# Down products h_hi·[w_hi | w_lo] 512 columns wide, their right half gated by ScalarE and added by GpSimd; another order at the projections' end

## Chip, cores, metric

One core of a Trainium2 chip runs the kernel. The metric is the device time of one execution in microseconds (us), the lower the better. The five engines are called TensorE (PE), VectorE (DVE), ScalarE (ACT), GpSimd (POOL) and SyncE (SP, which only issues transfers here).

## What is computed

One decoder layer on a float32 input x of 16 x 128 x 256 (16 batches, 128 positions, 256 features), with three blocks, each followed by a residual sum and a layer norm:

```python
x = layernorm(x + attention(x))        # q, k, alpha: 512 wide; v: 256 wide; a scan over the 128 positions
x = layernorm(x + experts(x, ctx, itok))
x = layernorm(x + ffn(x))              # 256 -> 1024 (two, silu gate) -> 1024 -> 1024 -> 256

def experts(x, weights, ensembles, proj_in, proj_out):   # E = 8 experts, hidden 512
    h = relu(einsum('edi,bsi->bsed', proj_in, x))
    o = einsum('eid,bsed->bsei', proj_out, h)
    gate = einsum('bks,bkse->bse', weights, one_hot(ensembles, E))
    return einsum('bsei,bse->bsi', o, gate)
```

All 8 experts are computed for every token, and each output row is multiplied by its gate.

## The kernel before

**Split products.** TensorE multiplies in the format fp32r. To keep float32 accuracy, each operand is stored as a high part (the value rounded to fp32r) and a low part (the rest), and each product is three matmuls: hi·hi, lo·hi and hi·lo, summed in one PSUM bank. `three()` lists them and `product()` issues them. High parts come from ScalarE (a copy that rounds), low parts from GpSimd or VectorE (a subtraction).

**Every engine's order is written out by hand.** Each engine has one in-order program, and they meet only at counting semaphores (`wait_ge`, `then_inc`). An instruction that waits holds everything behind it on its engine. Tokens are handled as t = 0..15 (a batch of 128 rows each), in groups g of J = 4.

**Projections (11 to 90 us).** For each token TensorE computes alpha, q and k (18 matmuls of 512 columns), in banks 0 to 2 or 3 to 5 by the token's parity; `values(g)` computes v for a whole group, after token 1 in group 0 and after the first token of the others, and needs the low parts of all four tokens of its group. The high and low parts of x for token t + 4 are made in turn t: `high_half` on ScalarE and `low_half` on GpSimd stood behind the other work of the turn. VectorE adds the bias (L1000), sums softplus (`a_sum`) and q·k (`b_sum`); ScalarE does abs, exp, ln and copies q and k out of PSUM; GpSimd multiplies q·k (L490).

**Tables (90 to 112 us).** The sums of a and b are transposed by TensorE, a chain of short VectorE operations makes one coefficient for each row (`c_tok`), rows are added and normed (`residual`, `norm_means`), while TensorE does the output products of attention. Behind them TensorE issues IDLE = 36 products of a unit matrix that nobody reads (L810), and then transposes the normed rows of group 0 (`turned(0)`, L816, L817).

**Experts (114 to 481 us).** 32 units, each one expert for one group of 4 tokens. `up` makes one of 4 chunks (128 hidden features x 512 tokens) of a unit's hidden layer: 6 matmuls of 512 columns (L741), in bank 0 or 1. ScalarE's `relu` writes the high part hx_hi (L647), VectorE's `low` the low part hx_lo (L1123). `down` makes the 128 x 256 output of one token: for each of the 4 chunks hi·hi, hi·lo, lo·hi of 256 columns (L845), in bank 2 or 3 by parity. VectorE's `gated` multiplies it by the gate and adds it to the token's row in x_tok (L1130). TensorE alternates: up of the next unit's chunk c, down of this unit's token c. Before `up` of chunk c TensorE waits for `low` of chunk c - 2; before `down` of token j for `gated` of token j - 2.

The first 8 units go group by group through experts 0 and 1 (`step`, two units per step, to 217 us). Meanwhile VectorE sums, norms and splits the later groups (`rows_added`, `norm_apply`, `halves_x`) and makes gates (L968). The other 24 go by pairs of experts (`pair`, 8 units each). There VectorE also takes in a piece of the next block's weights in the first two turns of a unit (`take_piece`: L1174 copy, L1176 compare) and makes one gate per turn (not in the last pair). Twice a pair ScalarE rounds the weights of the coming expert (`expert_high`, after units 1 and 5), and GpSimd subtracts them into wx_lo in four pieces (`expert_low`, L507). GpSimd had nothing else to do here except a root (`root`, L510) per group.

**Feed forward (481 to 806 us)**, in 4 groups, then the last norm and the output.

## Time and profile before

| | |
|---|---|
| median of 3 runs | 816.55 us (815.99 to 817.0) |
| the profiled execution | 814.71 us |
| its span, first to last instruction | 812.8 us |
| TensorE busy | 790.0 us (97%) |
| VectorE, ScalarE, GpSimd busy | 457.9, 306.5, 102.6 us |
| mean granted TensorE clock | 0.998 |

A matmul's record is longer than the time it takes of the engine, as matmuls overlap; what one costs is the distance between the starts of two in a row. The busy time of an engine counts overlapped time once.

### The profile page before, as it was taken

The page shows a single profiled execution, that of the slowest core. Times are in us where ns is not written, and L with a number is a line of the kernel's source. Part 1 is how long each engine was busy: PE and PEld are TensorE (multiplying, and loading weights), DVE is VectorE, ACT ScalarE, POOL GpSimd, SP SyncE. Part 2 cuts the span into 40 slices and gives each one's busy share as a digit, 9 for nine tenths or more (in the row PEclk, how much of TensorE's full clock was granted, in tenths as well). Part 3 has the DMA queues.
Part 4 walks back from the last instruction along what each step waited for, and adds up shares of the span by engine and source line. Part 5 has one row for each costly group of instructions (what it writes and reads, how often), then busy time and mean ns, then how long its engine had stood idle before and what let it go on. Part 6 is the DMA issues. An engine that isn't in the chain of part 4 may idle for free.

```text
span 812.8 us, 12974 instructions
## 1 busy us (share of the span) xinstructions
PE 790.0 (97%) x4414; PEld 689.5 (85%) x4414; DVE 457.9 (56%) x1122; ACT 306.5 (38%) x551; POOL 102.6 (13%) x102
## 2 busy tenths in 40 slices
PE   5999899999999999999999999999999999999996
PEld 4877789999999998999999988888888888888885
DVE  3677858886576676767666554324532453245214
ACT  6677632222232322323232235432643264326331
POOL 3676230001120100202020000000000000000000
PEclk9999999999999999999999999999999999999999
DMA  8500000000412122121311000000000000000000
GB/s 328 203 2 0 1 1 2 2 1 27 130 36 95 53 78 73 44 91 52 104 45 46 15 7 0 1 1 7 19 0 0 6 19 0 0 6 21 0 1 29
DMA packets 15587, 31.46 MB, mean 39 GB/s; under 512 B 1584, under 2 KB 6064, under 8 KB 15280
## 3 DMA queue, kind: packets, MB, share of 16 engines
q1 hardware_dynamic: 15536, 30.82, 11.7%
q8 instruction: 27, 0.44, 0.2%
q14 instruction: 24, 0.20, 0.1%
HBM read 28.72 MB, written 2.10 MB: 38 GB/s over the span
## 4 chain that ended last, share of the span: by engine, by line
PE 93%; DVE 3%; issue 2%; DMA 1%; ACT 1%; SPq 0%; POOL 0%; DVEq 0%; POOLq 0%
PE bank L741 37%; PE bank L921 29%; PE bank L845 22%; PE bank L936 3%; PE bank L810 1%; DMA wp_lo_f<-in_wproj 1%; DVE hx_lo L1123 0%; PE bank L864 0%; PE bank L865 0%; PE bank L817 0%; DVE xT_lo L1118 0%; PE bank L816 0%; DVE xf_lo L1192 0%; DVE sp L975 0%; DVE b_tok L983 0%
## 5 line engine op out<-in xcount | busy, mean ns | idle before, releaser
L647 ACT ACTIVATE hx_hi<-bank 128x512 fp32r<-128x512 f32 x128 | 76.7, 599 | 262.9 <-PE bank L741 262.8
L845 PE MATMUL bank<-wx_hi,hx_lo 128*128 128x256 f32 x512 | 144.9, 283 | 0.0
L845 PE MATMUL bank<-wx_lo_r,hx_hi 128*128 128x256 f32 x512 | 144.8, 283 | 0.0
L845 PE MATMUL bank<-wx_hi,hx_hi 128*128 128x256 f32 x512 | 144.3, 282 | 0.0
L1123 DVE SCALAR_TENSOR_TENSOR hx_lo<-bank,hx_hi 128x512 fp32r<-128x512 f32 x128 | 88.3, 690 | 86.5 <-ACT hx_hi L647 86.1
L741 PE MATMUL bank<-xT_hi,wx_hi 128*128 128x512 f32 x256 | 101.7, 397 | 2.2 <-DVE xT_lo L1118 1.3
L845 PEld LDWEIGHTS bank<-wx_hi,hx_hi 128*128 128x128 f32 x512 | 97.7, 191 | 5.3
L845 PEld LDWEIGHTS bank<-wx_lo_r,hx_hi 128*128 128x128 f32 x512 | 97.7, 191 | 4.9
L741 PE MATMUL bank<-xT_lo,wx_hi 128*128 128x512 f32 x256 | 101.1, 395 | 0.0
L921 PE MATMUL bank<-ha_hi_r,wf_hi_r 128*128 128x512 f32 x256 | 100.1, 391 | 0.0
L921 PE MATMUL bank<-hb_hi_r,wf_hi_r 128*128 128x512 f32 x256 | 99.9, 390 | 0.0
L921 PE MATMUL bank<-ha_lo,wf_hi_r 128*128 128x512 f32 x256 | 99.7, 390 | 0.0
L741 PE MATMUL bank<-xT_hi,wx_lo_r 128*128 128x512 f32 x256 | 99.7, 389 | 0.0
L921 PE MATMUL bank<-hb_lo,wf_hi_r 128*128 128x512 f32 x256 | 99.6, 389 | 0.0
L845 PEld LDWEIGHTS bank<-wx_hi,hx_lo 128*128 128x128 f32 x512 | 97.7, 191 | 0.0
L1228 DVE TENSOR_TENSOR ha_lo<-hf,ha_hi_r 128x512 fp32r<-128x512 f32 x64 | 44.0, 688 | 93.2 <-ACT hf L717 92.6
L1130 DVE SCALAR_TENSOR_TENSOR x_tok<-bank,gates,x_tok 128x256 f32<-128x256 f32 (+1 forms) x128 | 61.6, 481 | 18.5 <-PE bank L845 12.1
L1228 DVE TENSOR_TENSOR hb_lo<-hf,hb_hi_r 128x512 fp32r<-128x512 f32 x32 | 22.1, 692 | 78.2 <-ACT hf L717 78.2
L507 POOL TENSOR_TENSOR wx_lo_r<-wx_lo_f,wx_hi 128x512 fp32r<-128x512 f32 x28 | 36.6, 1335 | 220.5 <-ACT wx_hi L624 220.5
L741 PEld LDWEIGHTS bank<-xT_hi,wx_lo_r 128*128 128x128 f32 x256 | 48.1, 188 | 11.0
L921 PEld LDWEIGHTS bank<-ha_hi_r,wf_hi_r 128*128 128x128 f32 x256 | 48.1, 188 | 11.0 <-DVE ha_lo L1228 1.1
L921 PEld LDWEIGHTS bank<-ha_lo,wf_hi_r 128*128 128x128 f32 x256 | 48.1, 188 | 9.9
(151 smaller groups left out, 1339.2 us busy)
## 6 DMA issues: line engine op xcount, KB each, us to landing
stage<-in_wffn SPq DMA_DIRECT2D x44, 256.0 KB, 2.6
wx_lo_f<-in_wx SPq DMA_DIRECT2D x16, 512.0 KB, 3.9
xs_lo_f<-in_xT SPq DMA_DIRECT2D x4, 512.0 KB, 5.6
x_tok<-in_x SPq DMA_DIRECT2D x1, 2048.0 KB, 10.6
out<-x_tok SPq DMA_DIRECT2D x16, 128.0 KB, 1.7
wp_lo_f<-in_wproj SPq DMA_DIRECT2D x3, 512.0 KB, 6.9
ctx_sb<-in_ctx SPq DMA_DIRECT2D x1, 1024.0 KB, 8.5
itok_sb<-in_itok SPq DMA_DIRECT2D x1, 1024.0 KB, 10.4
```

Of the source, the lines that this page charges most:

```text
L507: pool.tensor_tensor(wx_lo[:, e, a], wx_raw[:, e, a], wx_hi[:, e, a].bitcast(F32), ALU.subtract).then_inc(s_wxlo_ok, 1)
L647: act.activation(hx_hi[:, place, c], bank[b][:, :], ACT.Relu).then_inc(s_relu_ok, 1)
L741: mm = pe.matmul(dst, a, b, start=(n == 0), stop=(n == len(pairs) - 1))
L810: pe.matmul(bank[0][:, 0:P], ident[:, :], ident[:, :], start=True, stop=True)
L845: mm = pe.matmul(bank[2 + j % 2][:, 0:D], x_, w_, start=(c == 0 and i == 0), stop=(c == XC - 1 and i == 2))
L921: mm = pe.matmul(bank[m % 4][:, :], wf[:, o + k * F + m * P:o + k * F + m * P + P], part[:, k], start=(k == 0 and i == 0), stop=(k == FC - ...
L936: mm = pe.matmul(bank[4 + j][:, 0:D], part[:, k, a], wf[:, W3 + k * D:W3 + k * D + D], start=(k == 0 and i == 0), stop=(k == FC - 1 and i ...
L1123: dve.scalar_tensor_tensor(out=hx_lo[:, place, c], in0=bank[b][:, :], scalar=0.0, in1=hx_hi[:, place, c].bitcast(F32), op0=ALU.max, op1=AL ...
L1130: dve.scalar_tensor_tensor(out=group_row(g, j), in0=bank[2 + j % 2][:, 0:D], scalar=gate, in1=group_row(g, j), op0=ALU.mult, op1=ALU.add). ...
L1228: dve.tensor_tensor(dst[:, m], hf[:, n % 3], hi[:, m].bitcast(F32), ALU.subtract).then_inc(s_f_lo, 1)
```

## The change

1. `down` issues for each chunk one matmul of 512 columns, h_hi·[w_hi | w_lo], into the whole bank, and one of 256 columns, h_lo·w_hi, into its left half. Before it issued three of 256 columns into the left half.
2. So each token has a second half to deal with. VectorE's `gated` still gates and adds the left half. Then ScalarE's `right_half` reads the right half from PSUM, times the gate, into a new buffer `right` in SBUF, and GpSimd's `right_added` adds it to the row of x_tok. `right_half` waits for `gated` of the same token and for `right_added` of the token two before; `right_added` waits for `right_half`; `gated` waits for `right_added` of the same row in the unit before; `down` waits for `right_half` of two tokens before.
3. GpSimd's pieces of `expert_low` are spread over the turns of units 2 and 6 of a pair, each behind a `right_added`; its roots, and the reduction over partitions, stand between them as well.
4. At the end of the last unit ScalarE's `keep(0)` and `norm2_T(0)`, which prepare the feed forward block, stand behind `right_half` of the third token, where they had been behind nothing of that unit.
5. In the projections `high_half` and `low_half` come first in a turn (but in group 0). In the last group TensorE makes alpha of tokens 14 and 15 first, then q and k of 14, then of 15; VectorE and ScalarE take both chunks of v in the second turn, and ScalarE does exp and ln of token 15 ahead of the copy of k of token 14.
6. IDLE is 12 where it was 36. The first group's row sums are issued one ahead of the statistics. At the very end VectorE scales the first two rows behind the means of the fourth.

```diff
-IDLE = 36
+IDLE = 12
...
             def down(unit, place, e, j, expert):
                 wo_h = wx_hi[:, e, OUT].rearrange("p (c d) -> p c d", c=XC)
-                wo_l = wx_lo[:, e, OUT].rearrange("p (c d) -> p c d", c=XC)
+                wo_hl = wx_both[:, :, e, OUT].rearrange("p h (c d) -> p h c d", c=XC)
                 if j == 0:
                     pe.wait_ge(s_wxlo_ok, expert * 4 + 4)
                 pe.wait_ge(s_gated_ok, unit * J + j + 1)
+                pe.wait_ge(s_right_ok, unit * J + j + 1)
...
-                    for i, (x_, w_) in enumerate(three(hx_hi[:, place, c, a], hx_lo[:, place, c, a], wo_h[:, c], wo_l[:, c])):
-                        mm = pe.matmul(bank[2 + j % 2][:, 0:D], x_, w_, start=(c == 0 and i == 0), stop=(c == XC - 1 and i == 2))
+                    if c > 0:
+                        pe.matmul(bank[2 + j % 2][:, 0:D], hx_lo[:, place, c, a], wo_h[:, c], start=False, stop=False)
+                    mm = pe.matmul(bank[2 + j % 2][:, :].rearrange("p (h d) -> p h d", h=2), hx_hi[:, place, c, a], wo_hl[:, :, c],
+                                   start=(c == 0), stop=(c == XC - 1))
+                    if c == 0:
+                        pe.matmul(bank[2 + j % 2][:, 0:D], hx_lo[:, place, c, a], wo_h[:, c], start=False, stop=False)
...
+            def right_added(unit, g, j):
+                pool.wait_ge(s_right_ok, unit * J + j + 3)
+                row = x_tok[:, g * J + j]
+                pool.tensor_tensor(row, right[:, j % 2], row, ALU.add).then_inc(s_row_ok, 1)
...
             def pair(p, last):
-                expert_low(1, p * 2 + 1)
-                if not last:
-                    expert_low(0, p * 2 + 2)
-            pairs_of_experts(pool, pair)
+                for u in range(8):
+                    for j in range(J):
+                        right_added(p * 8 + u, u % G, j)
+                        if u == 2:
+                            expert_low(1, p * 2 + 1, (j,))
+                        if u == 6 and not last:
+                            expert_low(0, p * 2 + 2, (j,))
+                    if u == 5 and last:
+                        ln_rstd(s_f_ve, s_f_rstd, 1)
+                        pool.wait_ge(s_wide_c, 1)
+                        pool.partition_all_reduce(wide_all[:, :], wide_col[:, :], P, RMAX).then_inc(s_wide_a, 1)
...
+            def right_half(unit, g, j, expert):
+                act.wait_ge(s_gated_ok, unit * J + j + 3)
+                act.wait_ge(s_row_ok, unit * J + j + 3)
+                gate = gates[:, bass.ds(g * J + j, 1), bass.ds(expert, 1)].rearrange("p b e -> p (b e)")
+                act.activation(right[:, j % 2], bank[2 + j % 2][:, D:2 * D], ACT.Copy, scale=gate).then_inc(s_right_ok, 1)
...
             def step(g, front):
                 for c in range(XC):
                     relu(g * 2 + 1, 1, c, c % 2)
+                    right_half(g * 2, g, c, 0)
                     if c == 1:
                         if front:
                             halves_x(g + 1)
...
             def pair(p, last):
                 for u in range(8):
-                    if u < 7 or not last:
-                        for c in range(XC):
+                    for c in range(XC):
+                        if u < 7 or not last:
                             relu(p * 8 + u + 1, (u + 1) % 2, c, c % 2)
+                        if u == 7 and last and c == 3:
+                            keep(0)
+                            norm2_T(0, True)
+                        right_half(p * 8 + u, u % G, c, p * 2 + u // G)
...
             def project(g, first, last):
                 for j in range(J):
                     t = g * J + j
+                    if not first and not last:
+                        low_half(t + J)
...
+            for t, n in ((B - 2, 0), (B - 1, 0), (B - 2, 1), (B - 2, 2), (B - 1, 1), (B - 1, 2)):
+                project(t, n)
...
                         summed(2)
-                        scaled((0, 1), G)
                         means((2,))
                         summed(3)
                         means((3,))
+                        scaled((0, 1), G)
```

## Rows read from the trace of the kernel before

**Rows 1.** The chain that ended last: its shares of the span by line.
```profile
by line: PE bank L741 37.5%; PE bank L921 28.7%; PE bank L845 22.0%; PE bank L936 3.3%; issue 1.5%; PE bank L810 1.0%; DMA wp_lo_f<-in_wproj 0.8%; DVE hx_lo L1123 0.3%; PE bank L864 0.2%; PE bank L865 0.2%; PE bank L817 0.2%; DVE xT_lo L111
```

**Rows 2.** Page: granted TensorE clock in 40 slices, in tenths.
```profile
PEclk9999999999999999999999999999999999999999
```

**Rows 3.** Windows: stretch, length, busy (instructions) of PE, PEld, DVE, ACT, POOL; clock; DMA.
```profile
217.00:481.00 264.00, 263.14 (x1694) 239.45 (x1693) 179.55 (x466) 67.50 (x119) 27.85 (x22) 1.00 0.20 59
```

**Rows 4.** The chain in order of time: start, us, what.
```profile
11.80 41.14 PE bank L741 x180
...
127.37 1.39 PE bank L741 x6
128.76 1.43 PE bank L845 x12
```

**Rows 5.** Timeline, PE, then POOL: start, us, operation, idle before; waits of PE.
```profile
53.75 0.47 PE L741 MATMUL bank<-xs_hi,wp_hi 128*128 128x512 f32 x1 [0.81 <-issue]
...
52.48 1.18 POOL L474 TENSOR_TENSOR xs_lo_r<-xs_lo_f,xs_hi  x1
...
PE bank L741 <- issue: 1.6, 2, 0.8
```

**Rows 6.** Timeline at the projections' end: ACT, POOL, DVE.
```profile
85.53 0.59 ACT L601 ACTIVATE k_sb<-bank 128x512 f32<-128x512 f32 x1
...
86.19 1.30 POOL L490 TENSOR_TENSOR qk<-q_sb,k_sb 128x512 f32<-128x512 f32 x1 [1.37 <-ACT k_sb L601]
...
92.45 0.69 DVE L983 TENSOR_REDUCE b_tok<-qk 128x8 f32<-128x512 f32 x1
```

**Rows 7.** Timeline ahead of the experts: PE, DVE, PE.
```profile
103.91 8.20 PE L810 MATMUL bank<-ident 128*128 128x128 f32 x72
...
106.02 1.38 DVE L1112 TENSOR_SCALAR x_tok<-x_tok,mv,rstd 128x256 f32<-128x256 f32 x4 [1.59 <-issue]
...
111.95 0.27 PE L816 MATMUL bank<-ident,x_tok 128*128 128x128 f32 x1
```

**Rows 8.** Groups by form (ACT: busy us, mean ns); one line's durations (POOL: min/median/max ns).
```profile
L634 ACT ACTIVATE u_sb<-bank 128x256 f32<-128x256 f32 x12 | 4.3, 382 | 4.6 <-PE bank L741 4.6
...
L474 POOL TENSOR_TENSOR xs_lo_r<-xs_lo_f,xs_hi x16: 723/752/1194, 7.0 to 72.6; 128x256 fp32r<-128x256 f32 x8, - x8
```

**Rows 9.** Timeline of DVE in the second half of a step.
```profile
135.16 0.69 DVE L1123 SCALAR_TENSOR_TENSOR hx_lo<-bank,hx_hi 128x512 fp32r<-128x512 f32 x1 [0.76 <-ACT hx_hi L647]
...
136.74 0.47 DVE L1130 SCALAR_TENSOR_TENSOR x_tok<-bank,gates,x_tok 128x256 f32 x1
```

**Rows 10.** Timeline, POOL and DVE: a GpSimd operation beside two gates.
```profile
196.59 2.60 POOL L507 TENSOR_TENSOR wx_lo_r<-wx_lo_f,wx_hi 128x512 fp32r<-128x512 f32 x2 [26.34 <-ACT wx_hi L624]
...
197.24 0.81 DVE L968 SCALAR_TENSOR_TENSOR masked_late<-itok_sb,expert_no,ctx_sb 128x128 f32<-128x128 int32 x1
197.98 1.37 DVE L968 SCALAR_TENSOR_TENSOR masked_late<-itok_sb,expert_no,ctx_sb 128x128 f32<-128x128 int32 x1
```

**Rows 11.** Timeline of DVE: one turn of a pair with GpSimd idle.
```profile
318.78 0.48 DVE L1130 SCALAR_TENSOR_TENSOR x_tok<-bank,gates,x_tok 128x256 f32<-128x256 f32 x1
...
319.74 0.69 DVE L1176 SCALAR_TENSOR_TENSOR stage<-stage,wf_hi_r 128x512 f32<-128x512 f32 x1
...
320.69 0.69 DVE L1123 SCALAR_TENSOR_TENSOR hx_lo<-bank,hx_hi 128x512 fp32r<-128x512 f32 x1
```

**Rows 12.** Timeline at the experts' end: ACT, DVE, PE.
```profile
474.61 1.39 ACT L669 ACTIVATE x_tok<-xn 128x256 f32<-128x256 f32 x4 [1.67 <-DVE xn L1112]
476.87 1.21 ACT L677 ACTIVATE xf_hi_r<-bank 128x256 fp32r<-128x256 f32 x4 [0.87 <-PE bank L865]
...
478.95 0.48 DVE L1130 SCALAR_TENSOR_TENSOR x_tok<-bank,gates,x_tok 128x256 f32<-128x256 f32 x1 [1.82 <-PE bank L845]
...
480.90 0.49 PE L741 MATMUL bank<-xf_hi_r,wf_hi_r 128*128 128x512 f32 x1 [0.55 <-DVE xf_lo L1192]
```

**Rows 13.** Timeline of DVE near the end.
```profile
806.08 0.72 DVE L1278 TENSOR_SCALAR x_tok<-x_tok,mv,rstd 128x256 f32<-128x256 f32 x2
```

More of the change, by code:

```diff
@@ L490, in project @@
                         pool.tensor_tensor(qk[:, j % 2], q_sb[:, j % 2], k_sb[:, j % 2], ALU.mult).then_inc(s_qk_ok, 1)
-                    if not last:
+                    if first:
                         low_half(t + J)
                     at = j - (2 if first else 1)
-                    if 0 <= at < DC:
+                    if last:
+                        for c in range(DC if j == 1 else 0):
+                            low_v(g * DC + c, g, c)
+                    elif 0 <= at < DC:
                         low_v(g * DC + at, g, at)
@@ L518, in _, with step @@
             expert_low(1, 1)
-            def step(g, front):
-                if front:
-                    root(g + 1)
-            steps(pool, step)
-            expert_low(0, 2)
-            def pair(p, last):
-                expert_low(1, p * 2 + 1)
-                if not last:
-                    expert_low(0, p * 2 + 2)
-            pairs_of_experts(pool, pair)
-            def ln_rstd(sem_in, sem_out, n, a=slice(0, J)):
-                pool.wait_ge(sem_in, n)
-                pool.tensor_tensor(rstd[:, a], var_eps[:, a], neghalf[:, a], ALU.pow).then_inc(sem_out, 1)
-            ln_rstd(s_f_ve, s_f_rstd, 1)
-            pool.wait_ge(s_wide_c, 1)
-            pool.partition_all_reduce(wide_all[:, :], wide_col[:, :], P, RMAX).then_inc(s_wide_a, 1)
+            def step(g, further, last):
+                for j in range(J):
+                    right_added(g * 2, g, j)
+                    if last and j == 1:
+                        expert_low(0, 2, (0, 1))
+                for j in range(J):
+                    if further and j == J - 1:
+                        root(g + 2)
+                    right_added(g * 2 + 1, g, j)
+                    if last and j == 1:
+                        expert_low(0, 2, (2, 3))
+            root(1)
+            for g in range(G - 1):
+                step(g, g < G - 2, False)
+            step(G - 1, False, True)
+            def pair(p, last):
+                for u in range(8):
+                    for j in range(J):
+                        right_added(p * 8 + u, u % G, j)
[7 more added lines that the diff above has]
+                        pool.partition_all_reduce(wide_all[:, :], wide_col[:, :], P, RMAX).then_inc(s_wide_a, 1)
+            for p in range(1, E // 2):
+                pair(p, p == E // 2 - 1)
             pool.wait_ge(s_wide_f, 1)
@@ L601, in project @@
                         act.activation(k_sb[:, r], bank[r * 3 + 2][:, :], ACT.Copy).then_inc(s_k_out, 1)
-                    if not last:
-                        act.wait_ge(s_x0T_in, 16 * g + 32)
+                    if first:
+                        act.wait_ge(s_x0T_in, 32)
                         high_half(t + J)
                     at = j - (2 if first else 1)
-                    if 0 <= at < DC:
+                    if last:
+                        for c in range(DC if j == 1 else 0):
+                            high_v(g * DC + c, g, c)
+                    elif 0 <= at < DC:
                         high_v(g * DC + at, g, at)
@@ L687, in pair @@
                         expert_high(0, p * 2 + 2)
-                    if u == 7 and last:
-                        keep(0)
-                        norm2_T(0, True)
             pairs_of_experts(act, pair)
@@ L1003, in project @@
                         b_sum(t - 1, 1 - r)
+                    if j == J - 2 and last:
+                        dve.wait_ge(s_a_mm, t + 2)
+                        dve.tensor_tensor(al[:, 1 - r], bank[(1 - r) * 3][:, :], bias_b[:, :], ALU.add).then_inc(s_al_out, 1)
                     if j == 1 and not first and not last:
@@ L1012, in project @@
                     at = j - (2 if first else 1)
-                    if 0 <= at < DC:
+                    if last:
+                        for c in range(DC if j == 1 else 0):
+                            take_v(g * DC + c, c)
+                    elif 0 <= at < DC:
                         take_v(g * DC + at, at)
```

100 lines of the change are left out of this document (70 added, 30 removed).

## Prediction

> **What bounds the kernel now.** I read the chain of waits first. It is TensorE's nearly throughout: projections, up and output products (L741) 37.5%, feed forward (L921) 28.7%, down products (L845) 22.0% [rows 1]. The clock row shows the full clock, the 2.4 GHz level, in every slice [rows 2], so nothing is to be won there. The windows tell what the others have left: in the 264 us of the pairs TensorE has no gap to speak of (263.14 busy), VectorE is busy for 179.55, ScalarE for 67.50, GpSimd for 27.85 [rows 3]. So an instruction less on TensorE counts in full, if the work moved to the other three doesn't hold TensorE. In the order of time the chain gives TensorE's pace: an up of 6 matmuls 1.39 us, a down of 12 matmuls 1.43 us, so a turn of 2.82 us [rows 4]. The gaps and the stretches between the blocks I took from the timeline.
>
> **1. The down products.** 12 matmuls in 1.43 us are 119.5 ns for each of 256 columns. One of 512 columns costs 1.39/6 = 231 ns here and 41.14/180 = 228.6 ns in the projections [rows 4]. A chunk is now one of each: 0.348 to 0.351 us where it was 0.358. A down becomes 1.394 us (mean), 0.04 less, and 32 x 4 = 128 of them save 5.1 us. The columns stay the same; what goes is the fixed part of one matmul in three. No row shows this mix, or a 512-column moving operand in two runs far apart. Bounds: if the second half of the wide one costs what a 256-column matmul costs, nothing is saved; if the narrow one after it costs half of a wide one (115 ns), 7 us. I take 5.1, as both parts have rows.
>
> The Trainium skill (TensorE: Matmul & The Clock Gate, section Back-to-back issue gap) gives N/2.4 + 2.5 ns per matmul at the full clock. By it, as an estimate, only 4 x 2.5 ns go from a down, 1.3 us in all, and so the change would win a quarter of my figure. The measured 119.5 and 229 ns are above its 109 and 216, and the fixed part that they show is larger, so I go by the rows.
>
> **2. Projections.** TensorE stops before `values(2)` from 52.8 to 53.75 us, behind the low part of token 11, which GpSimd begins only at 52.48 [rows 5]; it is put down to "issue". The waits list such a stop twice with 0.8 each [rows 5], about 0.95 each from start to start with the weight load. With `low_half` and `high_half` first in the turn that low part is made about 3 us sooner: -1.9 us.
>
> **3. The projections' end and the tables.** The chain to the tables ends with b_tok, written at 93.1 us [rows 6]. The rows of the new order laid end to end make it longer, not shorter. VectorE now takes both chunks of v before al(14), which starts at 83.5 instead of 82.3, and al(15) ends at 86.7. ScalarE's abs(15) waits for that, and q(14), ln(14), exp(15) and ln(15) then stand ahead of the copy of k(14): it starts at about 89.5, where it was 85.53 [rows 6]. GpSimd's q·k of token 14 (1.30) follows, and behind it on VectorE b_sum(14), a_sum(15), q·k(15), b_sum(15): b_tok at 94.8, +1.7 us for everything up to the output products. The row sums issued one ahead give back 0.9 on VectorE alone.
> Then IDLE. Its 72 records cover 8.20 us, 114 ns each, to 111.95, when the first transpose starts; but the normed rows are there from 106.02 to 107.4 [rows 7]. With 12 products the block takes 2.73 us. TensorE comes to the transposes at 103.91 + 1.7 + 2.73 = 108.35, VectorE's rows at 106.02 + 1.7 - 0.9 = 106.8 to 108.2. So 111.95 becomes 108.35, -3.6 us; with no loss at the projections' end -5.3. ScalarE's `expert_high` and GpSimd's pieces are done in time there.
>
> **4. The steps (group by group).** ScalarE is in order, so this ring closes: relu(c+1) waits behind `right_half`(c), that for `gated`(c), that stands on VectorE behind `low` and the row sums, and `low` waits for relu(c). Its length: relu 0.60 + 0.03, then 136.74 - 135.16 = 1.58 from `low` to `gated` [rows 9], then 0.48 of `gated` itself, then ScalarE's part. A copy of 256 columns out of PSUM took 0.38 us [rows 8]; with a gate per row I take 0.38 to 0.42 busy, 0.35 to the next. That is 3.04 or more against the turn of 2.78. Before, the ring was open: relu waited for TensorE alone. In the second halves of steps 0 and 1 it loses 0.3 per turn, then the means and `norm_apply` follow on the same queue, and `halves_x` stands on ScalarE behind `right_half`(1). Laid end to end a step's TensorE waits 0.4 at the second down, 0.5 at the transposes, 0.9 at the next up for xT_lo; with 0.3 in the first step 3.9 us, and 5.0 if `right_half` is 0.06 longer. I take +4.7; from below, the shortest form without any of the lag gives 0.
>
> **5. The pairs.** GpSimd and VectorE hold each other up. At 196.59 a GpSimd subtraction runs, the gate at 197.24 takes 0.81 us instead of 0.35, and the next one, back to back with it, 1.37: GpSimd's second piece went in between [rows 10]. Operations of VectorE with one operand in PSUM are not touched. In a turn with a weight piece the compare (L1176) starts 0.96 us after `gated` [rows 11]; `right_added` starts 0.48 + 0.03 + 0.38 + 0.08 = 0.97 after it, nearly a tie, and takes 0.75 [rows 8]. Whoever loses, VectorE gets some 0.7 us more in such a turn: the turn's 320.69 - 318.78 = 1.91 us [rows 11], 0.61 for `low` and 0.7 make 3.2 us against 2.78, for two turns in four, and catches up in the others. TensorE sees that only where `expert_low` comes too: units 2 and 6 of pairs 1 and 2, four in all. If `right_added` is first, the piece of 1.25 us stands between compare and gate, VectorE's turn is 4.4 us, and two of them in a row, less 0.8 of slack, hold TensorE for 2.5 us: 10 us in all. If the compare is first, the piece runs beside `low` and `gated` and costs 0 to 1 per unit. Between 0 and 12, I take +5.
>
> The Trainium skill (SBUF — State Buffer, section SBUF: two separate sides) says that VectorE with two SBUF inputs and GpSimd take an exclusive lock for a whole instruction, which the trace bears out with the 1.37 us above. It speaks against handing these sums to GpSimd.
>
> **6. The experts' end.** `keep(0)` and `norm2_T(0)` (1.39 and 1.21 us [rows 12]) now start only after `right_half` of the third token. `gated` of it starts at 478.95 [rows 12], `right_half` ends 0.9 later at 479.9, then 2.6 us, then 0.4 of VectorE: TensorE starts the feed forward at 482.9 to 483.3 in place of 480.90 [rows 12]. GpSimd's long reduction in unit 6 delays `right_added`, so ScalarE and one down by about 0.5. Together +2.9.
>
> **7. The last rows.** VectorE's scaling of two rows (0.72 [rows 13]) goes behind the last means, while GpSimd makes the last root; the last row ends about 0.2 earlier, but all four outputs go out within 1.3 us. +0.2, between -0.2 and +1.
>
> **Sum.** -5.1 - 1.9 - 3.6 + 4.7 + 5 + 2.9 + 0.2 = +2.2 us. Against the profiled execution's own 814.7 that is 816.9; the median of the runs shown lies 1.84 above that execution, so 818.8.
>
> **Rivals.**
> a) The three engines hide their new work (faster). The point that decides it is the tie of part 5 going to the compare and the ring of part 4 staying under a turn. Then parts 4 and 5 are at most 2, and the sum is -5.1 - 1.9 - 3.6 + 2 + 2.9 + 0.2 = -5.5: 813. For it: ScalarE is idle for three quarters of the pairs and GpSimd for nine tenths [rows 3], and VectorE's row shows 0.3 us to spare even in its fullest turn. Against: the ring's 3.04 us come from rows.
> b) The tie goes to `right_added` throughout: part 5 is 10 to 12, the sum +7 to +9, 825. For it: 0.97 and 0.96 can't be told apart. With parts 1 and 3 as they are, this is clearly slower.
> c) The wide matmul brings nothing, as its second half costs what a matmul of 256 columns costs: +5.1 on top, 824. It decides if a down stays at 1.43 us. Against it: an up's matmul of 512 columns is 8 ns shorter than two of 256, and the 228.6 ns of the projections hold `values` too, whose moving operand lies in four runs.
> By the figure of the page on TensorE in the Trainium skill (part 1) this rival would hold by three quarters, as an estimate +3.8.
> d) With fewer idle products the clock falls to 1.2 GHz before the experts. TensorE would have had gaps of about 1 us only, beside products, so I hold this for unlikely; at the 1.2 GHz level the 3 us from the transposes to the first up would cost 1.5 more, 820.
>
> **How the numbers follow.** My forecast, both mechanisms in part, 0.45; a) 0.30; b) 0.15; c) 0.07; d) 0.03. The likeliest is 818.8, by itself 816 to 822. The range takes in a) and b): 811.5 to 827. A difference of 0.2%, 1.6 us, is about what a measurement of this kernel can tell from none. Faster than 814.9: a) nearly whole and a little of the forecast, 0.33. Within: 0.17, from the low side of the forecast. Slower than 818.2: 0.50.
>
> **What will show it.** Down at 1.39 us in the chain (part 1). No stop before `values(2)` and `values(3)`; b_tok near 93 (that is 94.8 - 1.9); the first transpose near 106.5 with the last idle product just ahead of it. In the steps, ups behind `xT_lo` and a relu put down to ScalarE's own queue. In the pairs, gates and compares of over 1 us, and waits of TensorE for hx_lo at four units only. A wait of about 3 us before the feed forward. I am wrong if VectorE's compare doesn't lengthen, or if the ring's turn stays at 2.78; and at part 3 if k(14) is copied early.

## The result and the profile after

The changed kernel takes 828.77 us (median of 4 runs, 827.29 to 829.27), the kernel before 816.61 us in the same comparison (815.99 to 817.0): a ratio of 1.0147, with a 95% interval from 1.0129 to 1.0164. The profiled execution took 828.8 us and its span is 827.0, 14.2 more than the span of before. The forecast was 818.8, between 811.5 and 827.0: the direction was right, the size was not, and the time lies outside the range.

Lines of the changed kernel's profile are its own: up products L805, down products L912, L913 and L916, `right_half` L707, `right_added` L521, GpSimd's reduction over the partitions L567.

The page of the changed kernel, granted clock in 40 slices. One slice has fallen, which no slice had before [rows 2]:

```profile
PEclk9999999999999999999999969999999999999999
```

The chain in order of time, in a quiet unit of the pairs (start, us, what):

```profile
220.95 1.36 PE bank L805 x6
...
223.72 1.36 PE bank L805 x6
...
226.48 1.36 PE bank L805 x6
```

From up to up is 2.77 us, where an up and a down took 2.82 before [rows 4]. That is the gain, and it is larger than forecast. Of the 0.053 us only half lies in the down (2.77 - 1.36 = 1.41 us, where it was 1.43): the other half lies in the up, 1.36 us instead of 1.39, although its six matmuls are the same in both kernels. TensorE's waits (engine and line, for whom: us in total, times, longest) say where it is lost:

```profile
PE bank L913 <- ACT right L707: 9.7, 5, 7.5
...
PE bank L805 <- DVE xT_lo L1209: 3.5, 4, 1.3
PE bank L805 <- DVE xf_lo L1284: 2.7, 1, 2.7
...
PE bank L805 <- POOL wx_both L527: 1.1, 2, 0.6
```

One wait of 7.5 us for `right_half` is more than half of the whole loss. The timeline around it, POOL, then ACT, then PE (start, us, operation, in brackets the idle time before it and who ended it):

```profile
465.48 1.02 POOL L516 TENSOR_TENSOR rstd<-var_eps,neghalf 128x4 f32<-128x4 f32 x1 [0.70 <-DVE var_eps L1114]
472.43 0.38 POOL L567 PARTITION_ALL_REDUCE wide_all<-wide_col  x1 [5.94 <-issue]
479.99 2.09 POOL L521 TENSOR_TENSOR x_tok<-right,x_tok 128x256 f32<-128x256 f32 x3 [7.18 <-issue]
...
480.80 0.47 ACT L707 ACTIVATE right<-bank,gates 128x256 f32<-128x256 f32 x1 [10.35 <-POOL x_tok L521]
...
481.53 0.76 PE L913 MATMUL bank<-wx_both,hx_hi 128*128 128x512 f32 x1 [7.54 <-ACT right L707]
...
489.74 0.48 ACT L707 ACTIVATE right<-bank,gates 128x256 f32<-128x256 f32 x1 [1.82 <-DVE x_tok L1222]
490.11 1.32 ACT L732 ACTIVATE x_tok<-xn 128x256 f32<-128x256 f32 x4
...
493.30 0.64 PE L805 MATMUL bank<-xf_hi_r,wf_hi_r 128*128 128x512 f32 x1 [2.71 <-DVE xf_lo L1284]
```

GpSimd's reduction itself lasts 0.38 us. But it begins 5.94 us after the instruction ahead of it ended, and the next `right_added` begins 7.18 us after it; both times are "issue", not a wait for another engine. GpSimd is away from 466.5 to 480.0. `right_added` of three tokens is then done in one go, ScalarE had waited 10.35 us, TensorE 7.54.

The windows around it (length, busy time and instructions of PE, PEld, DVE, ACT, POOL; granted clock; DMA share; GB/s):

```profile
465.00:473.00 8.00, 8.00 (x42) 6.81 (x42) 3.70 (x10) 2.15 (x4) 1.40 (x2) 1.00 0.00 0
473.00:481.50 8.50, 0.98 (x6) 0.57 (x5) 0.00 (x0) 0.70 (x2) 1.51 (x3) 0.70 0.09 15
481.50:490.00 8.50, 8.47 (x38) 7.42 (x39) 4.30 (x10) 1.94 (x5) 2.80 (x4) 0.70 0.00 0
490.00:493.00 3.00, 0.58 (x3) 0.21 (x2) 1.26 (x4) 2.53 (x9) 0.74 (x1) 1.00 0.00 0
493.00:497.00 4.00, 3.70 (x9) 2.97 (x10) 0.55 (x2) 0.47 (x1) 0.73 (x1) 0.57 0.02 4
497.00:501.00 4.00, 4.00 (x19) 3.26 (x19) 1.79 (x3) 3.54 (x5) 0.00 (x0) 1.00 0.00 0
```

A granted clock of 1.00 is the 2.4 GHz level, 0.50 the 1.2 GHz level; 0.70 and 0.57 are means over a window that holds both. After the wait the clock is at its 1.2 GHz level for two downs, and after the second wait, of 2.7 us, again: 9 matmuls of the feed forward in the window from 493 to 497, and 19 in the next one, which is as long.

The steps, ScalarE's `right_half` of four tokens in a row (the row at 145.49 comes behind the means, that at 149.20 behind the norming), then two of TensorE's waits:

```profile
138.34 0.48 ACT L707 ACTIVATE right<-bank,gates 128x256 f32<-128x256 f32 x1 [2.21 <-DVE x_tok L1222]
...
141.52 0.47 ACT L707 ACTIVATE right<-bank,gates 128x256 f32<-128x256 f32 x1 [2.22 <-DVE x_tok L1222]
...
145.49 0.47 ACT L707 ACTIVATE right<-bank,gates 128x256 f32<-128x256 f32 x1 [3.01 <-DVE x_tok L1222]
...
149.20 0.48 ACT L707 ACTIVATE right<-bank,gates 128x256 f32<-128x256 f32 x1 [2.56 <-DVE x_tok L1222]
...
142.25 0.47 PE L913 MATMUL bank<-wx_both,hx_hi 128*128 128x512 f32 x1 [0.24 <-ACT right L707]
...
146.11 0.47 PE L913 MATMUL bank<-wx_both,hx_hi 128*128 128x512 f32 x1 [0.83 <-ACT right L707]
```

The turns are 3.18, 3.97 and 3.71 us against TensorE's 2.77.

Last, the projections' end and the transposes (ACT, POOL, DVE, then PE), beside [rows 6, 7]:

```profile
89.26 0.58 ACT L651 ACTIVATE k_sb<-bank 128x512 f32<-128x512 f32 x1
...
89.91 1.30 POOL L498 TENSOR_TENSOR qk<-q_sb,k_sb 128x512 f32<-128x512 f32 x1 [4.17 <-ACT k_sb L651]
...
93.87 0.69 DVE L1055 TENSOR_REDUCE b_tok<-qk 128x8 f32<-128x512 f32 x1
...
105.33 2.84 PE L876 MATMUL bank<-ident 128*128 128x128 f32 x24
108.01 0.27 PE L882 MATMUL bank<-ident,x_tok 128*128 128x128 f32 x1
```

One thing lies ahead of all this. The two profiled executions differ at their start, where both kernels do the same work. The windows of the kernel before, then of the changed one:

```profile
12.00:14.00 2.00, 2.00 (x10) 1.55 (x10) 2.00 (x3) 0.38 (x1) 0.00 (x0) 1.00 1.03 428
14.00:16.00 2.00, 2.00 (x10) 1.68 (x9) 0.32 (x1) 1.61 (x3) 0.00 (x0) 1.00 1.01 422
```

```profile
12.00:14.00 2.00, 2.00 (x5) 1.61 (x6) 2.00 (x3) 0.41 (x1) 0.00 (x0) 1.00 1.01 420
14.00:16.00 2.00, 2.00 (x7) 1.53 (x7) 0.36 (x1) 1.58 (x3) 0.00 (x0) 1.00 1.02 426
```

Matmuls start 0.43 us apart instead of 0.23 for about 3.5 us longer, as they would at half the clock, although the row has 1.00 in both. The 24th matmul begins at 15.80 before and at 17.57 after, so 1.77 of the 14.2 us are not the change's. (The 1.84 us that the forecast's sum adds to get from the profiled execution of before to the median are of the same size; only profiled executions show their start.) Over all profiles of this study that start lies at 15.8 to 15.95 in three (the kernel before is one) and at 17.4 to 18.4 in eleven, whatever the kernel. In experiment 4, which is the kernel before with two idle additions on GpSimd, it lies at 18.18, 2.4 later, and the span is 815.2, 2.4 longer than the 812.8 of before. Below, "with the start set apart" means that a trace's times are taken less this difference.

The account, trace against trace:

| where | forecast | measured |
|---|---|---|
| start, not the change's | 0 | +1.8 |
| 128 turns, a down and an up each (part 1) | -5.1 | -6.8 (0.053 each, 0.025 of it in the down) |
| to the first transpose (parts 2, 3) | -5.5 | -5.7 (-3.94 in the traces) |
| steps (part 4) | +4.7 | +7.3 |
| pairs (part 5) | +5 | +3.4 |
| experts' end (part 6) | +2.9 | +12.4, and +1.8 of slow clock behind it |
| last rows (part 7) | +0.2 | 0 |
| sum | +2.2 | +14.2 |

The +12.4 are 7.54 of the wait, 2.71 - 0.55 = 2.2 before the feed forward, and 2.4 for two downs at the low clock (5.2 us from 481.53 to 486.73, where two take 2.8); 0.3 were not placed. With the start set apart the loss is 14.2 - 1.8 = 12.4 us, beside 12.2 by the medians. The steps' and pairs' figures are the lengths of 4 turns of each unit against 4 x 2.77 and against before's own excess.

### The profile page after: what moved, and what is told of

Same layout as the page of the kernel before. It is cut to its first block, busy times and chain, and to the rows that moved or that the text cites. A ratio compares the mean times of both kernels' runs of the same rounds, so it can differ in the third digit from the quotient of the medians.

```text
span 827.0 us, 12504 instructions
## 1 busy us (share of the span) xinstructions
PE 788.3 (95%) x3854; PEld 660.8 (80%) x3854; DVE 466.4 (56%) x1122; ACT 358.7 (43%) x679; POOL 208.9 (25%) x230
## 4 chain that ended last, share of the span: by engine, by line
PE 79%; DVE 7%; issue 7%; ACT 3%; POOL 1%; DVEq 1%; DMA 1%; ACTq 0%; SPq 0%; POOLq 0%
PE bank L805 31%; PE bank L993 28%; PE bank L913 10%; PE bank L912 4%; PE bank L1008 3%; DVE x_tok L1222 1%; ACT hx_hi L700 1%; PE bank L916 1%; DVE hx_lo L1214 1%; DVE x_tok L1123 1%; DMA xs_lo_f<-in_xT 1%; POOL x_tok L521 1%; DVE xT_lo L1209 1%; ACT wx_both L677 0%; ACT right L707 0%
## 5 line engine op out<-in xcount | busy, mean ns | idle before, releaser
L913 PE MATMUL bank<-wx_both,hx_hi 128*128 128x512 f32 x512 | 193.7, 401 | 9.7 <-ACT right L707 9.7
L805 PE MATMUL bank<-xT_hi,wx_both 128*128 128x512 f32 x512 | 180.0, 393 | 6.0 <-DVE xT_lo L1209 3.5
L521 POOL TENSOR_TENSOR x_tok<-right,x_tok 128x256 f32<-128x256 f32 x128 | 107.9, 844 | 221.5 <-ACT right L707 214.2
L707 ACT ACTIVATE right<-bank,gates 128x256 f32<-128x256 f32 x128 | 60.9, 476 | 220.8 <-DVE x_tok L1222 210.5
L913 PEld LDWEIGHTS bank<-wx_both,hx_hi 128*128 128x128 f32 x512 | 97.1, 190 | 28.4 <-issue 9.1
L805 PEld LDWEIGHTS bank<-xT_hi,wx_both 128*128 128x128 f32 x512 | 96.3, 188 | 25.4 <-DVE xT_lo L1209 4.7
L912 PE MATMUL bank<-wx_both,hx_lo 128*128 128x256 f32 x384 | 109.1, 284 | 0.0
L805 PE MATMUL bank<-xT_lo,wx_both 128*128 128x512 f32 x256 | 99.8, 390 | 0.0
L912 PEld LDWEIGHTS bank<-wx_both,hx_lo 128*128 128x128 f32 x384 | 73.6, 192 | 5.3
L805 PEld LDWEIGHTS bank<-xT_lo,wx_both 128*128 128x128 f32 x256 | 48.1, 188 | 10.3
```

The costliest lines, as they stand in the source:

```text
L521: pool.tensor_tensor(row, right[:, j % 2], row, ALU.add).then_inc(s_row_ok, 1)
L707: act.activation(right[:, j % 2], bank[2 + j % 2][:, D:2 * D], ACT.Copy, scale=gate).then_inc(s_right_ok, 1)
L805: mm = pe.matmul(dst, a, b, start=(n == 0), stop=(n == len(pairs) - 1))
L912: pe.matmul(bank[2 + j % 2][:, 0:D], hx_lo[:, place, c, a], wo_h[:, c], start=False, stop=False)
L913: mm = pe.matmul(bank[2 + j % 2][:, :].rearrange("p (h d) -> p h d", h=2), hx_hi[:, place, c, a], wo_hl[:, :, c], start=(c == 0), stop=(c ...
```

## Experiments

All edits are to the changed kernel unless said. The kernel before ran beside each on the same chip, with medians of 816.2 us (experiments 1 to 4) and 816.4 us (5 to 12).

**1. The maximum without GpSimd.** VectorE's `wide_col` is transposed by TensorE in unit 6, and VectorE takes the maximum of the row.

```diff
-    pool.wait_ge(s_wide_c, 1)
-    pool.partition_all_reduce(wide_all[:, :], wide_col[:, :], P, RMAX).then_inc(s_wide_a, 1)
+    pe.transpose(bank[7][0:1, D:D + P], wide_col[:, :], ident[:, :]).then_inc(s_wide_a, 1)
...
+    dve.tensor_reduce(wide_all[0:1, :], bank[7][0:1, D:D + P], AX_X, ALU.max).then_inc(s_wide_m, 1)
```

> The changed kernel, but the maximum over the partitions that sets the flag is made by one transpose on TensorE and a row maximum on VectorE; nothing else differs. Theory: GpSimd's reduction over the partitions holds GpSimd for 13.5 us (466.5 to 480.0), and that costs TensorE its one wait of 7.54 us, and the lower clock behind it some 4 us more. Then right_added runs through, the wait goes, the clock stays at the full level, and the kernel takes 828.8 - 7.5 - 4 = 817 us. Rival 1: only the wait goes and the clock falls all the same, for another reason: 821. Rival 2: the wait is not the reduction's but that of the normed rows or of the weight pieces, which then comes up in its place: 827 to 829.

Measured: 819.06 us, ratio 1.0042 (1.003 to 1.0054). That is 9.7 less than the changed kernel, so of the 12.2 us lost four fifths came by this one instruction and the low clock behind it. The theory's 11.5 was 2 too high, since the second wait, before the feed forward, stays and brings its own low clock:

```profile
483.00:487.00 4.00, 3.43 (x9) 2.77 (x10) 0.83 (x3) 0.47 (x1) 0.74 (x1) 0.57 0.00 0
```

**2. `keep` one token earlier**, on top of 1.

```diff
-    if u == 7 and last and c == 3:
+    if u == 7 and last and c == 2:
         keep(0)
         norm2_T(0, True)
```

> As the one before (maximum by TensorE), and ScalarE's keep(0) and norm2_T(0) ahead of right_half of token 2 of the last unit instead of token 3. Theory: TensorE waits for xf_lo before the feed forward for 0.5 us instead of 2.7, because keep starts one right_half earlier, so 2.2 us less than the kernel beside it: 815. Rival: the right halves of tokens 2 and 3 come 2.6 us later and hold the last two downs instead, and the gain is 0 to 0.5.

Measured: 815.79 us, 0.9992 (0.998 to 1.0005): 3.3 less than 1. In this trace the wait is back at its old length, and the feed forward starts at full pace, which is the 1.1 us beyond the expected 2.2:

```profile
483.06 0.49 PE L804 MATMUL bank<-xf_hi_r,wf_hi_r 128*128 128x512 f32 x1 [0.58 <-DVE xf_lo L1287]
```

The two edits together bring the change from 12 us slower to no difference that can be measured.

**3. The right half left out.** TensorE makes the full products; `right_half` and `right_added` and the waits for them are not there, so the part of the output that they carry is missing.

> The changed kernel with the right half of each down product left out: TensorE still makes the products of 512 columns, but ScalarE doesn't gate the right half and GpSimd doesn't add it (this part of the sum is missing in the output), and GpSimd's reduction over the partitions stands as it is. Theory: all that the change costs behind the projections is the handing on of the right half, all that it gains is the 0.053 us of each down (6.8 us) and 3.9 us ahead of the experts. So no stall in the steps, the pairs and at the reduction: 816.6 - 6.8 - 3.9 = 805.9 us. Rival 1: part of the stalls in the steps comes from the new order of rows and idle products and stays: 808 to 811. Rival 2: the gain of a down was only the idle product's and the matmul of 512 columns gains 5.1: 807.6.

Measured: 802.49 us, 0.9844 (0.9822 to 0.9865), 3.4 below the expectation. The expectation had taken the front's gain as 3.9, the traces' difference, from which the late start had not been set apart; with 5.7 it is 816.2 - 6.8 - 5.7 = 803.7. The median still lies 1.2 below that; of its four runs three lie at 802.1 to 802.7, the profiled one with the early start among them, and one at 804.98. Its turns are 2.77; units 0, 2 and 4 have 2.99, and had 3.04 before, the same excess, and unit 16 has 2.87 (2.96 before). So neither the row sums nor the idle products cost anything new in the steps. The trace is 26.6 us shorter than the changed kernel's: 1.6 of that is the start, and the other 25 are the handing on of the right half, with what the reduction and the low clock make of it. Rivals 1 and 2 fall.

**4. What the reduction does to GpSimd**, in the kernel before, where nobody waits for it.

```diff
+    pool.tensor_tensor(stage_probe[:, 0:4], neghalf[:, :], neghalf[:, :], ALU.add)
     pool.partition_all_reduce(wide_all[:, :], wide_col[:, :], P, RMAX).then_inc(s_wide_a, 1)
+    pool.tensor_tensor(stage_probe[:, 4:8], neghalf[:, :], neghalf[:, :], ALU.add)
```

> The kernel before, with one tiny GpSimd addition (128x4) right ahead of the reduction over the partitions and one right behind it, with no wait of their own. Theory: GpSimd's next ordinary instruction after the reduction starts some 7.2 us after the reduction's end, whatever it is; the first addition also shows how long the reduction takes to begin (some 6 us). So the pair lies 13 to 14 us apart. TensorE doesn't wait for either: 816.6, as before. Rival: the 7.2 us in the changed kernel are a wait for right_half and for other engines, and the second addition starts within 0.5 us of the reduction's end.

Measured: 816.99 us, one run. The timeline of POOL:

```profile
468.36 0.20 POOL L540 TENSOR_TENSOR stage_probe<-neghalf 128x4 f32<-128x4 f32 x1
474.42 0.38 POOL L541 PARTITION_ALL_REDUCE wide_all<-wide_col  x1 [5.86 <-issue]
481.94 0.19 POOL L542 TENSOR_TENSOR stage_probe<-neghalf 128x4 f32<-128x4 f32 x1 [7.14 <-issue]
```

Two additions of 0.2 us with no wait of their own stand 13.4 us apart. The time on both sides of the reduction is GpSimd's, in the kernel before too; there the next instruction on GpSimd came 38 us later, so no row showed the second part. What GpSimd does in these two times no trace shows; and as an execution holds one such reduction, whether a second one would cost the same wasn't run. The Trainium skill (GPSIMD Engine Reference, section 4.1 Engine selection) gives reductions over the partitions to GpSimd; experiment 1 disagrees for one column with work queued behind it: TensorE's transpose and a row maximum did it with no wait that the trace shows.

**5. The right half by VectorE.** A second operation on the same bank, behind that for the left half; ScalarE and GpSimd do nothing for it. The reduction stays on GpSimd.

```diff
     dve.scalar_tensor_tensor(out=group_row(g, j), in0=bank[2 + j % 2][:, 0:D], scalar=gate, in1=group_row(g, j), ...
+    dve.wait_ge(s_gated_ok, unit * J + j + 3)
+    dve.scalar_tensor_tensor(out=group_row(g, j), in0=bank[2 + j % 2][:, D:2 * D], scalar=gate, in1=group_row(g, j),
+                             op0=ALU.mult, op1=ALU.add).then_inc(s_right_ok, 1)
```

> The changed kernel, but VectorE gates and adds the right half itself, in a second operation on the same PSUM bank behind that of the left half; ScalarE and GpSimd have no part in it. GpSimd's reduction over the partitions stays. Theory: the stalls come from handing the right half to ScalarE and then to GpSimd, in lock step with VectorE. VectorE pays 0.48 us more per down; in a turn of a pair it is then busy for 0.61 + 0.5 + 0.5 = 1.6 and with a weight piece 1.3 more, 2.9 against 2.77 in two turns of four, which the other two even out. In the steps' second halves 0.6 + 0.8 + 0.5 + 0.5 = 2.4 and the means, all under or near a turn, so 2 to 3 us of stalls in the steps, 0 to 1 in the pairs, none at the reduction, and xf_lo comes as early as before: 802.5 + 3 = 805 to 807 us. Rival: VectorE becomes the bound in the turns with weight pieces (0.15 us lost in each of 44, and more with the gates of the next experts): 812 to 818.

Measured: 807.04 us, 0.9885 (0.9869 to 0.9902), at the theory's upper end. Its turns are 2.77 in the pairs but for unit 16 (3.13; 2.97 before), and 2.98, 3.02 and 3.15 in units 0, 2 and 4. VectorE has the time for the second operation. The trace of experiment 3, without any right half, is 4.7 us shorter still: 2.0 of that is the start, 0.8 lies in the steps, 1.1 in unit 16, and 0.5 before the feed forward (a wait of 1.1 us).

**6. The gate ahead of the row work in the steps**, on top of 2.

```diff
+    gated(g * 2 + 1, g, c, 1)
     if further:
         rows_added(g + 2, c)
-    gated(g * 2 + 1, g, c, 1)
```

and in the same way ahead of `norm_apply`.

> The version with the maximum by TensorE and keep earlier (815.8), and in the steps VectorE gates the left half ahead of the row sum and statistics, and ahead of the norming, instead of behind them. Theory: in the steps the ring relu, low, row work, gate, right_half, relu lasts 3.18 us, 3.97 with the means in it and 3.7 with the norming, against TensorE's turn of 2.77. Without the row work in it the ring is under 2.5 us and open, and of the 7.3 us that the five units lose against their pace most goes; the waits for xT_lo (0.9 each) may stay: 815.8 - 4.5 = 811. Rival: VectorE's own load sets the steps' turn and the row work is only lost elsewhere (later rows, later transposes): within 1 us of 815.8.

Measured: 810.59 us, 0.9923 (0.9902 to 0.9944), 5.2 less than 2. The `right_half` rows of the same turns:

```profile
137.19 0.47 ACT L706 ACTIVATE right<-bank,gates 128x256 f32<-128x256 f32 x1 [1.90 <-DVE x_tok L1225]
...
140.04 0.47 ACT L706 ACTIVATE right<-bank,gates 128x256 f32<-128x256 f32 x1 [1.89 <-DVE x_tok L1225]
...
142.90 0.47 ACT L706 ACTIVATE right<-bank,gates 128x256 f32<-128x256 f32 x1 [1.89 <-DVE x_tok L1225]
```

2.85 us apart where they were 3.18 and 3.97. Over the whole of units 2 and 4 a turn takes 3.29 and 3.31 in place of 3.72 and 3.70. So the row work inside the ring is the cause of most of the loss in the steps; the 0.3 us a turn that these two units still have above experiment 3 wasn't taken apart.

**7. GpSimd's weight pieces ahead of `right_added`**, on top of 2.

```diff
-    right_added(p * 8 + u, u % G, j)
     if u == 2:
         expert_low(1, p * 2 + 1, (j,))
     if u == 6 and not last:
         expert_low(0, p * 2 + 2, (j,))
+    right_added(p * 8 + u, u % G, j)
```

> The version with the maximum by TensorE and keep earlier (815.8), and in the pairs each of GpSimd's expert_low pieces goes ahead of right_added of its turn instead of behind it. Theory: the 3.4 us that TensorE loses in the pairs at units 10, 14, 16, 18 and 22 come mainly from the last low piece being made too late, behind right_half and right_added of its turn; a piece ahead of it is there about 1 us sooner, and right_added itself has two turns of slack: 815.8 - 2 = 814. Rival: the stall is the shared port's (pieces running beside VectorE's operations with two operands in SBUF): then it only moves, and the time stays within 0.7 us of 815.8, or right_half comes late and it rises.

Measured: 813.88 us, 0.9969 (0.9957 to 0.9982), 1.9 less than 2. The wait for `wx_both` is gone from the trace; a turn takes 2.80 in unit 10 (2.95), 2.77 in units 14 and 22 (2.87), 2.93 in unit 18 (3.09), and 3.08 in unit 16 as before the edit (3.10). So more than half of what the pairs lost was the order on GpSimd's queue. What is left in units 16 and 18 wasn't taken apart.

**8. The old order of the projections' end**, on top of 2: TensorE, VectorE, ScalarE and GpSimd go through the last four tokens as in the kernel before; the row sums one ahead, the low parts first and the 12 idle products stay.

```diff
-for t in range(B - 2):
+for t in range(B):
     for n in range(3):
         project(t, n)
...
-for t, n in ((B - 2, 0), (B - 1, 0), (B - 2, 1), (B - 2, 2), (B - 1, 1), (B - 1, 2)):
-    project(t, n)
```

> The version with the maximum by TensorE and keep earlier (815.8), with the last group of the projections in the order of the kernel before on all four engines; the row sums one ahead, the low parts first in their turn and the 12 idle products stay. Theory: the new order lengthens the chain to the tables: k of token 14 is copied 3.7 us later, b_tok is complete 1.4 us later than before in spite of TensorE being 1.9 us ahead. With the old order b_tok comes at 92 or earlier, and the experts start 1.5 to 3 us earlier: 813 to 814.5. Rival: TensorE's outputs and idle products, not the tables, set the start of the experts, and the new order costs nothing: 815.8.

Measured: 813.36 us, 0.9964 (0.9952 to 0.9975), 2.4 less than 2. Its k of token 14 is copied at 85.04 instead of 89.26, and with the start set apart the first transpose is at 104.45, against 106.24 in the changed kernel: 1.8 us. The new order costs what the prediction's chain said (+1.7).

**9. VectorE for both halves, gate first, old end.**

> The version in which VectorE gates and adds both halves (807.0), with the gate ahead of the row work in the steps and with the last group of the projections in the order of the kernel before. Theory: its steps lose only 1 us to the row work, of which 0.3 goes; the old order brings the experts 1.9 us forward, as it did in the traces of the version with GpSimd once the start of the two executions is set apart: 807.0 - 0.3 - 1.9 = 804.8. Rival: with VectorE holding both halves, the two orders meet other waits (rows later, xT_lo later), and the time stays at 807.

Measured: 806.44 us, 0.9872 (0.9848 to 0.9897), 1.6 above the expectation. The old end brought its 1.8 us (transposes 1.8 earlier with the start set apart), but with both halves on VectorE the gate first is wrong: a turn of unit 2 is 3.29 instead of 3.02, of unit 4 3.23 instead of 3.15; experiment 12, without the gate first, has 3.01 and 3.16. That two gates ahead of the row work make the rows late is likely, but wasn't followed row by row.

**10. The kernel before with 12 idle products.** `IDLE = 36` becomes `IDLE = 12`, nothing else.

> The kernel before with 12 idle products instead of 36, nothing else. Theory: the transposes then wait for the normed rows; in the changed kernel the first transpose started 1.45 us after the norming began, so 106.02 + 1.45 = 107.5 instead of 111.95: 816.4 - 4.5 = 811.9. That the whole of the changed kernel's front brings no more than this would mean that its row sums ahead and its low parts first are eaten by the new order of the projections' end. Rival: the clock falls with fewer idle products, and half of it or more comes back: 814 or above.

Measured: 810.26 us, 0.9923 (0.9902 to 0.9943), more than expected. The timeline of PE:

```profile
106.39 2.84 PE L810 MATMUL bank<-ident 128*128 128x128 f32 x24
109.07 0.27 PE L816 MATMUL bank<-ident,x_tok 128*128 128x128 f32 x1
```

The transposes follow the idle products at once, as in the changed kernel, and don't wait for the rows, so the whole 24 x 2 records of 114 ns are won: with the start set apart 106.58 against 111.95 [rows 7], 5.4 us. The 1.45 us after the norming, on which the expectation rested, was set by the idle products and not by the norming. The granted clock stays at 1.00 there.

**11. The change's own division of work, with 1, 2, 6, 7 and 8 together.**

> The change's own division of the work (ScalarE gates the right half, GpSimd adds it) with all four mends: maximum by TensorE, keep earlier, gate ahead of the row work, low pieces ahead, old end of the projections. Theory: the mends act at different places and add up: 815.8 - 5.2 - 2 - 2 = 806.5, about as fast as the version with VectorE alone. Rival: what is left of the ring and of the shared port takes up part of it: 809 to 811.

Measured: 807.53 us, 0.9895 (0.9876 to 0.9914). 8.3 less than 2, where 6, 7 and 8 won 5.2 + 1.9 + 2.4 = 9.5 one by one: they act at different places and nearly add up. It is within 0.5 us of experiment 5, so the three engines can carry the right half almost as cheaply as VectorE, once the orders on their queues are right.

**12. VectorE for both halves, old end, the row work ahead of the gate.**

> The version in which VectorE gates and adds both halves (807.0), with the last group of the projections in the order of the kernel before, and the row work in the steps ahead of the gate as the change has it. Theory: in the trace of the version with both edits the old order brought the transposes 1.8 us forward and the gate first lost 1.2 of it again in units 2 and 4 (3.29 and 3.23 us a turn in place of 3.02 and 3.15). Without the gate first those turns are back at 3.02 and 3.15 and the time is 807.0 - 1.8 = 805.2, the fastest. Rival: the units lose as much because the experts start earlier against the same rows: 806.4, as the version with both.

Measured: 804.48 us, 0.9851 (0.9837 to 0.9864), 0.7 below the expectation and the fastest that computes the whole reference. No run has the edits ahead of the experts without the wide matmuls. From the traces, as an estimate: this one is 11.9 us shorter than before with the start set apart, 7.5 of it ahead of the first transpose, so some 4.4 us are left for the wide matmuls and the handing on of the right half together.

```profile
span 803.2 us, 12150 instructions
...
PE 780.5 (97%) x3854; PEld 658.6 (82%) x3854; DVE 514.1 (64%) x1250; ACT 306.5 (38%) x551; POOL 101.1 (13%) x102
```

VectorE is now the second engine at 64%, with ScalarE at 38% and GpSimd at 13%.

## Why the prediction was wrong

**The step that failed is in part 6:** "GpSimd's long reduction in unit 6 delays `right_added`, so ScalarE and one down by about 0.5." Measured were 7.54 us of wait and about 2.5 of low clock behind it, 9.7 with the reduction off GpSimd (experiment 1). The first half of the 13.4 us, "issue" of some 6 us ahead of the reduction, stood in the trace of before. The second half, 7.14 us behind it, could not be seen, since GpSimd had nothing to do there; this was an unknown cost, and it was given a value and no upper bound. The working also left out the clock: behind both long waits of this trace TensorE ran at the 1.2 GHz level. Without this step the rest would have come out at 828.77 - 9.7 = 819.1, beside a forecast of 818.8; that they agree is partly luck, as parts 1, 4 and 5 were off in both directions.

**Part 6, `keep` and `norm2_T`** behind `right_half`: forecast +2.4, measured +2.2, and another 1.1 through the clock (experiment 2).

**Part 1** had the right sign, a size too small, and a reason that covers only half of it. A turn is 0.053 us shorter, 6.8 us in all, but the down itself went from 1.432 to 1.407 us, 0.025 less and not 0.040: a chunk takes 0.352 us, at the top of the 0.348 to 0.351 from rows. (The mean of these two gives a down of 1.398, not the 1.394 that the sum used.) The other 0.028 us are the up's, 1.388 to 1.360, with matmuls that the change didn't touch. In the kernel before, the first of them start 229 to 236 ns apart; in experiment 3, and in both kernels in the projections and in the feed forward, 512-column matmuls start 227 ns apart. So the 231 ns on which the part rested were high for an up that comes behind twelve narrow matmuls; what slows it there, no run shows. Rival c) is out as a time, by this and by experiment 3; inside a down, though, a wide matmul takes 227 to 241 ns, little under the 239 of two narrow ones. The figure of the Trainium skill (TensorE: Matmul & The Clock Gate, section Back-to-back issue gap), 2.5 ns for a matmul, gave 1.3 us; the trace doesn't agree with it: with four matmuls less the down is 25 ns shorter, 6 ns for each, and the turn 53 ns, 13 ns for each.

**Parts 2 and 3** came out: -5.7 against -5.5. The stops before `values` are gone, the idle products end right ahead of the first transpose, the order of the projections' end costs 1.8 (experiment 8) against +1.7 forecast. b_tok ended at 94.56 less 1.77, that is 92.8, "near 93" as forecast. The gain is nearly all of IDLE (experiment 10, 5.4); the new order eats what the stops gave.

**Part 4:** the ring is as described, and closed: 3.18 us a turn where 3.04 "or more" was forecast, since `right_half` takes 0.476 us and not 0.38 to 0.42. The sum was 2.6 short, most likely because the two turns with the means and with the norming (3.97 and 3.71) were counted with too little for TensorE: 5.8 of the 7.3 are those of units 2 and 4. Experiment 6 shows the ring by opening it, experiment 5 by taking it away.

**Part 5:** the tie went to the compare, mostly, and the pairs lost 3.4 us instead of 5, at the four units forecast and at unit 16, which had 0.6 us of it before. What held TensorE was not a lengthened VectorE but GpSimd's piece behind `right_added`: with the order turned, 1.9 us come back (experiment 7). VectorE's compare didn't lengthen (0.77 us in the mean, 0.79 before), which the prediction had named as a sign of being wrong; the operation that makes a gate, behind it, did (0.56 us against 0.37), and the mean of `right_added` is 0.84 us against 0.75 alone. So the two engines do hold each other up, but what that cost VectorE didn't reach TensorE.

**The clock, rival d),** did not fall where it was looked for, before the experts, but behind a wait of 7.5 us and one of 2.7 us. Fewer idle products left it at 1.00.

**Rival a)** was summed wrongly: its -5.5 us give 816.55 - 5.5 = 811.0, not 813, just below the range's lower end of 811.5. It didn't come to pass, so nothing hangs on it here.

## What to carry to other kernels

When work is handed to an engine that seemed idle, look at every instruction on its queue in that stretch and at what stands behind each: an instruction of which the profile shows 0.4 us can keep the engine for 13, and that is only visible where something is queued behind it; if nothing is, give it an upper bound, not a guess. Three engines that pass each row on in turn make a ring whose length is the sum of its parts, and any row work that one of them does in between is part of it. Look then at the orders on the queues before the division of work is given up: here the same division took 829 us, and 807.5 with the orders mended and the reduction off GpSimd. Also ask whether the engine with the second longest queue can do the work alone: VectorE, at 0.48 us more a row, gave 807 us as it stood and 804.5 with the old end of the projections. Before a difference of two traces is explained, compare their starts, where both do the same.

## What was not expected of the hardware

- The reduction over the partitions on GpSimd: 5.94 us from the instruction ahead of it to its start, 0.38 us of its own, 7.18 us to the start of the next one in the changed kernel; 5.86, 0.38 and 7.14 in experiment 4; 5.75 and 0.38 in the kernel before, where nothing followed closely.
- TensorE's clock: during the wait of 7.5 us it fell to 0.50, its lower level, and it granted 0.70 in the mean over the 8.5 us behind it, after idling 2.7 us 0.57 over the window from 493 to 497; after 0.6 us it didn't fall, nor after the 1.27 us ahead of the experts. At the low level matmuls of 512 columns start 0.43 us apart, at the full one 0.23.
- At the start of an execution the same pace of 0.43 us lasts until about 12 us or until 15.4 us and more, in executions of any kernel, with a granted clock of 1.00 in the row. It moves a trace by 1.8 to 2.6 us, nearly as much as the runs of one kernel lie apart (814.2 to 817.2).
- The six 512-column matmuls of an up, the same in both kernels, take 1.388 us behind twelve of 256 columns and 1.360 us behind four of 256 and four of 512; why, no run shows. Each 256-column matmul that was folded into a wide one saved 13 ns, 6 of them in the down and 7 in the up.
